# The last tile of a gated attention block, multiplied on GpSimd in halves and turned inside the products of the tile ahead

## The chip, the cores and the metric

The kernel runs on one core of a Trainium2 chip. The metric is device time in microseconds (us) of one execution: 338.8 us median of three runs (338.32 to 339.88).

## The reference, cut to what matters

2048 tokens of width 256 pass through a gated cross attention (16 heads of 64, 64 keys) and then a mixture of 16 experts, two per token, at most 320 rows an expert:

```python
x = x + tanh(g_xattn[0]) * xattn(layernorm(x), ctx, gamma, beta, Wq, Wkv, Wo, bo, mask)
x = x + tanh(g_ffn[0]) * ffn(layernorm(x), gate_w, w1, w2)

def ffn(x, gate_w, w1, w2):          # capacity 320, sentinel = 16 * 320
    probs = sigmoid(xf @ gate_w.T)
    top_vals, sel = top_k(probs, 2)
    weights = top_vals / (top_vals.sum(-1, keepdims=True) + 1e-06)
    onehot = one_hot(sel.reshape(-1), E)
    ranks = take_along_axis(cumsum(onehot, axis=0), flat_sel[:, None], axis=1)[:, 0] - 1
    valid = ranks < capacity
    slot = where(valid, flat_sel * capacity + ranks, sentinel)
    padded = zeros((sentinel + 1, d)).at[slot].set(repeat(xf, 2, axis=0))[:sentinel].reshape(E, capacity, d)
    h = gelu(einsum('ecd,edf->ecf', padded, w1))
    out_padded = einsum('ecf,efd->ecd', h, w2).reshape(sentinel, d)
    return (where(valid, out_padded[slot], 0) * weights).reshape(T, 2, d).sum(1)
```

## The kernel before

The tokens are 16 tiles of 128 rows, numbered 0 to 15 (`LAST` is 15), and 8 pairs of tiles (`PAIRS`). The order of every engine is written out by hand; engines wait for each other on counting semaphores. A loop of steps (`steps`) runs tiles through a pipeline: in step s tile s is scored, tile s-1 gets its softmax factors, tile s-2 is turned and multiplied with the values, tile s-3 gets its residual, its second norm and its gate. After step 15 a tail, written out, brings tiles 13, 14 and 15 through. The experts follow, and TensorE (PE) is fed in them by three products of float32r halves (high and low parts) for every exact one.

Of one tile in the tail, in order:

- `normalise` (line 492, POOL) multiplies the exponentials `probs` by `norm`, the inverse row sums; for tile 15 this is line 1047, on DVE.
- `turn_probs` (1217, PE) turns them into `ps_pT`; `copy_probs` (606, ACT) takes the high part, `low_probs` (968, DVE) the low part of each half.
- `attend` (1269, PE) makes 24 products into `ps_out`; between them `router` (1256) of the tile ahead.
- `first_residual` (978, DVE) makes `x1`; `second_stats` (986) its mean and variance; `second_norm` (468 to 470, POOL) the inverse deviation and the shift, in three instructions that wait for each other.
- `turn_x1` (1248, PE), `copy_x1` (622, ACT) and `router` give the logits; `gate_exp` (630, ACT) takes their exponentials, scaled by the inverse deviation; `second_rows` (615, ACT) writes the normalised rows `z2`.
- `begin`, `find`, `choose`, `place` (991 to 1026, DVE) find the two experts of each row; `counts` and `count_one` (1283 to 1295, PE) give the ranks. Tiles 12 and 13 (pair 6) go together, tile 14 and tile 15 each alone.
- `dispatch` (460, POOL) sends the rows to `padded` in DRAM by indirect DMAs, 4 for a pair. SP fetches an expert's rows back (378 to 381) when all of them have landed.

PE then issues 40 filler matmuls (1193, `keep_busy(40)`), turns the first expert's rows (1354), issues 8 more fillers and starts the first product (1370). ACT and DVE split the first weights meanwhile; DVE's first of these waits for `rows_sent` (540), POOL's mark behind its last dispatch.

## Time and profile before

| what | value |
|---|---|
| median of the runs | 338.8 us (338.32 to 339.88) |
| the profiled execution | 339.9 us, span 338.2 us |
| mean granted clock of PE | 0.968 of full |
| busy share of PE, DVE, ACT, POOL | 91%, 74%, 61%, 57% |
| end of step 15's products, start of the first expert product | 155.5 us, 188.7 us |

All positions below are in us from the span's start. In the timelines a row stands for one instruction or several alike ("x12"), with the time from the first's start to the last's end; the idle time ahead of it and what ended it follow in brackets. Matmuls overlap, so the next row can start before the one above ends. PEclk 0.50 is 1.2 GHz, 1.00 is 2.4 GHz.

### The profile page before, as it was taken

The page shows a single profiled execution, that of the slowest core. Times are in us where ns is not written, and L with a number is a line of the kernel's source. Part 1 is how long each engine was busy: PE and PEld are TensorE (multiplying, and loading weights), DVE is VectorE, ACT ScalarE, POOL GpSimd, SP SyncE. Part 2 cuts the span into 40 slices and gives each one's busy share as a digit, 9 for nine tenths or more (in the row PEclk, how much of TensorE's full clock was granted, in tenths as well). Part 3 has the DMA queues.
Part 4 walks back from the last instruction along what each step waited for, and adds up shares of the span by engine and source line. Part 5 has one row for each costly group of instructions (what it writes and reads, how often), then busy time and mean ns, then how long its engine had stood idle before and what let it go on. Part 6 is the DMA issues. An engine that isn't in the chain of part 4 may idle for free. (4 is left out here: it accounts for less than half of the span.)

```text
span 338.2 us, 6265 instructions
## 1 busy us (share of the span) xinstructions
PE 308.3 (91%) x2077; PEld 267.3 (79%) x2080; DVE 251.2 (74%) x585; ACT 207.9 (61%) x570; POOL 191.4 (57%) x242
## 2 busy tenths in 40 slices
PE   8989999999999999998849999999999999999800
PEld 3646779988888888887724899999999999999700
DVE  2679887698989898989755398888888888887200
ACT  2646877887888888866461376666666666665300
POOL 8034566585777777788771023555555555566650
PEclk9999999999999999999978999999999999999965
DMA  6989999700111111111224737878787878853440
GB/s 159 274 241 292 182 167 152 195 19 16 49 49 55 57 57 64 56 51 62 78 95 149 249 104 201 204 205 208 204 216 211 224 202 220 211 82 43 48 46 8
DMA packets 40906, 45.68 MB, mean 135 GB/s; under 512 B 5461, under 2 KB 34666, under 8 KB 40874
## 3 DMA queue, kind: packets, MB, share of 16 engines
q1 hardware_dynamic: 33410, 35.78, 39.3%
q0 software_dynamic: 7424, 9.48, 15.6%
q8 instruction: 17, 0.28, 0.4%
q14 instruction: 15, 0.12, 0.2%
q10 hardware_dynamic: 40, 0.02, 0.0%
HBM read 28.02 MB, written 17.24 MB: 134 GB/s over the span
## 5 line engine op out<-in xcount | busy, mean ns | idle before, releaser
L554 POOL DMA_INDIRECT out_dram<-wqT,diag x48 | 73.3, 1528 | 77.4 <-DMA out_dram<-wqT,diag 43.4
L1370 PE MATMUL ps_scores<-value_t,score_t 128*128 128x320 f32 x384 | 59.1, 310 | 0.0
L1370 PEld LDWEIGHTS ps_scores<-value_t,score_t 128*128 128x128 f32 x384 | 56.5, 188 | 0.4 <-DVE value_t L1079 0.3
L1269 PE MATMUL ps_out<-value_t,pT 128*128 128x256 f32 x384 | 53.3, 289 | 0.9 <-DVE pT L968 0.9
L1240 PE MATMUL ps_scores<-score_t,xn 128*128 128x512 f32 x192 | 53.9, 426 | 0.0
L1269 PEld LDWEIGHTS ps_out<-value_t,pT 128*128 128x128 f32 x384 | 47.7, 189 | 1.7 <-issue 1.6
L1240 PEld LDWEIGHTS ps_scores<-score_t,xn 128*128 128x128 f32 x192 | 36.4, 190 | 6.8
L713 ACT ACTIVATE ps_scores<-ps_scores 128x640 f32<-128x640 f32 x30 | 20.6, 688 | 34.2 <-PE ps_scores L1370 34.1
L460 POOL DMA_INDIRECT padded<-z,slot_row x32 | 33.4, 1043 | 10.0 <-issue 7.1
L640 ACT ACTIVATE probs<-ps_scores,row_low 128x64 f32<-128x64 f32 x128 | 38.0, 327 | 0.5 <-DVE row_low L941 0.5
L1093 DVE CAST value_t<-ps_scores 128x640 fp32r<-128x640 f32 x30 | 24.7, 824 | 18.0 <-ACT ps_scores L713 17.8
L492 POOL TENSOR_TENSOR probs<-probs,norm 128x1024 f32<-128x1024 f32 x15 | 28.6, 1906 | 5.5 <-DVE norm L909 5.5
L640 ACT ACTIVATION_READ_ACCUMULATOR probs<-ps_scores,row_low 128x1 f32 x128 | 28.4, 222 | 0.0
L848 DVE TENSOR_TENSOR pT<-ps_pT,pT 128x512 fp32r<-128x512 f32 x28 | 18.5, 660 | 5.2 <-ACT pT L606 4.9
L1095 DVE TENSOR_TENSOR value_t<-ps_scores,value_t 128x512 fp32r<-128x512 f32 x30 | 20.8, 692 | 1.0
L1106 DVE TENSOR_TENSOR score_t<-raw,score_t 128x1024 fp32r<-128x1024 f32 x16 | 19.4, 1216 | 2.6 <-POOL sent L540 2.6
L1193 PE MATMUL ps_misc<-zeros 128*128 128x512 bf16 x62 | 18.8, 461 | 1.5 <-DVE zeros L805 1.2
L1079 DVE TENSOR_TENSOR value_t<-ps_pT,value_t 128x640 fp32r<-128x640 f32 x16 | 13.1, 816 | 8.2 <-ACT value_t L701 8.2
L606 ACT ACTIVATE pT<-ps_pT 128x512 fp32r<-128x512 f32 x32 | 18.0, 644 | 0.9 <-PE ps_pT L1217 0.9
L701 ACT ACTIVATE value_t<-ps_pT 128x640 fp32r<-128x640 f32 x16 | 11.3, 706 | 11.9 <-PE ps_pT L1354 11.7
L630 ACT ACTIVATE gexp<-ps_scores,l 128x16 f32<-128x16 f32 x16 | 4.4, 276 | 22.3 <-PE ps_scores L1256 16.7
L483 POOL CAST xn<-xn_full 128x256 fp32r<-128x256 f32 x16 | 6.4, 399 | 20.6 <-ACT xn_full L654 20.5
(210 smaller groups left out, 690.0 us busy)
## 6 DMA issues: line engine op xcount, KB each, us to landing
raw<-in_L_ffn_w_dram SPq DMA_DIRECT2D x16, 512.0 KB, 4.8
wo_sb<-in_L_ffn_w_dram SPq DMA_DIRECT2D x16, 512.0 KB, 3.5
padded<-empty SPq DMA_DIRECT2D x2, 2064.0 KB, 31.0
diag<-padded SPq DMA_DIRECT2D x16, 258.0 KB, 4.9
out_dram<-x SPq DMA_DIRECT2D x16, 128.0 KB, 1.7
padded<-empty SPq DMA_DIRECT2D x1, 1032.0 KB, 34.1
diag<-padded SPq DMA_DIRECT2D x16, 64.5 KB, 4.7
wq_sb<-in_L_xattn_Wq_dram SPq DMA_DIRECT2D x2, 512.0 KB, 8.0
```

The costliest lines, as they stand in the source:

```text
L460: pool.indirect_dma_start(padded, bass.IndirectOffsetOnAxis(ap=slot_row[:, r % 2, k, q:q + 1], axis=0), z2[:, (2 * r + k) % RING, q], None ...
L492: pool.tensor_tensor(probs[:, p], probs[:, p], norm[:, p, :, None].to_broadcast([P, HEADS, KEYS]), ALU.mult).then_inc(normed, 1)
L554: pool.indirect_dma_start(out, bass.IndirectOffsetOnAxis(ap=xg[0:SLOTS[k], r, k, TOKEN:TOKEN + 1].bitcast(U32), axis=0), y[0:SLOTS[k], j, ...
L640: op = act.activation(probs[:, j, n], ps_scores[:, 1, at:at + KEYS], ACT.Exp, scale=-1.0, bias=row_low[:, n:n + 1], accum_out=row_sum[:, j ...
L713: act.activation(h_at(t, h), ps_scores[:, 2 * h:2 * h + 2, 0:CAPACITY], ACT.Gelu).then_inc(h_act, 1)
L1093: dve.tensor_copy(h_high_of(p)[:, fs], h_at(t, h)).then_inc(h_high, 1)
L1095: dve.tensor_tensor(h_low_of(p)[:, fs], h_at(t, h)[:, :, 0:n], h_high_of(p)[:, fs, 0:n].bitcast(F32), ALU.subtract)
L1106: dve.tensor_tensor(w1_hl(p, 1), raw1[:, p], w1_hl(p, 0).bitcast(F32), ALU.subtract).then_inc(w1_low, 1)
L1193: pe.matmul(ps_misc[:, :], idle_rows[:, 0:P], idle_rows, start=True, stop=True)
L1240: op = pe.matmul(dst, xn[:, t % 2, a, c], mv, start=False, stop=last)
L1269: op = pe.matmul(ps_attn, pT[:, a, c], mv, start=c == 0 and (a, b) == PARTS[0], stop=c == HC - 1 and (a, b) == PARTS[-1])
L1370: op = pe.matmul(ps_scores[:, f, 0:CAPACITY], w1_hl(p, a)[:, c, f * P:(f + 1) * P], x_hl(p, b)[:, c], start=c == 0 and (a, b) == PARTS[0], ...
```

## The change

- Tile 15's multiply moves from DVE (one of 1024 columns) to POOL (two of 512), each half with its own inverse and factor.
- Tile 15 is turned between the products 4 and 5 of tile 14's eight groups, into a buffer of its own (`score_t`), and its products go to a bank of their own (`ps_misc`), so that they needn't wait for tile 14's residual. The counts of pair 6 stand ahead of tile 14's last group. The router of tile 13 stands ahead of tile 14's products. Fillers go from 5 and 3 to 2.
- From tile 12 on the second norm is on three engines: DVE makes -mean and variance + eps (two instructions more behind its aggregate), POOL only the power, ACT the product (`shift`, a 128x1 activation) ahead of `second_rows`.
- On DVE the residual of tile 14 moves behind pair 6's places, the weights behind the choice (`weigh`), that of tile 15 behind `find`.
- POOL's dispatches stand in another order around the norms and multiplies.
- The 64 rows of expert 0's third block are fetched on ACT's DMA queue; the 0.5 KB rest has a semaphore of its own (`tailed`) for which PE doesn't wait.

```diff
+        pT_last = score_t[:, 0:2 * HC * P].rearrange("p (k c n) -> p k c n", k=2, c=HC)
+        shift = sb("shift", [P, 2, 1])
-        ps_attn = ps_out[:, 0:DIM]
+        def attn_of(t):
+            return ps_misc[:, 0:DIM] if t == LAST else ps_out[:, 0:DIM]
+        LATE_TILE = 2 * LATE_PAIR + 2
...
@@ sync: fetch(e)
-                    sp.dma_start(xg[0:SLOTS[2], r, 2], padded[at + 2 * P:at + CAPACITY, :]).then_inc(fetched[r], 16)
-                    sp.dma_start(xg[SLOTS[2]:, r, 2, TOKEN:], padded[at + 2 * P:at + CAPACITY, TOKEN:]).then_inc(fetched[r], 16)
+                    if e > 0:
+                        sp.dma_start(xg[0:SLOTS[2], r, 2], padded[at + 2 * P:at + CAPACITY, :]).then_inc(fetched[r], 16)
+                    sp.dma_start(xg[SLOTS[2]:, r, 2, TOKEN:], padded[at + 2 * P:at + CAPACITY, TOKEN:]).then_inc(tailed[r], 16)
...
@@ gpsimd: second_norm(t)
                 pool.wait_ge(stats2_ready, t + 1)
+                if t >= LATE_TILE:
+                    pool.tensor_tensor(l2[:, p, 1:2], l2[:, p, 0:1], power[:, 0:1], ALU.pow).then_inc(ln2_ready, 1)
+                    return
...
+            def last_multiply(h):
+                p, at = LAST % 2, 8 * h
+                pool.wait_ge(norm_ready, TILES + h)
+                pool.tensor_tensor(probs[:, p, at:at + 8], probs[:, p, at:at + 8],
+                                   norm[:, p, at:at + 8, None].to_broadcast([P, 8, KEYS]), ALU.mult).then_inc(normed, 1)
...
@@ scalar: second_rows(t)
+                if t >= LATE_TILE:
+                    bias = shift[:, p]
+                    act.activation(bias, l2[:, p, 2:3], ACT.Copy, scale=l2[:, p, 1:2]).then_inc(shifted, 1)
+                    act.wait_ge(shifted, t - LATE_TILE + 1)
...
@@ scalar: expert(e), e == -1
+                    for k in range(2):
+                        act.wait_ge(dispatched[k], 64 * PAIRS // 2)
+                    act.dma_start(xg[0:SLOTS[2], 0, 2], padded[2 * P:CAPACITY, :]).then_inc(fetched[0], 16)
...
@@ vector
+            def second_stats(t):
+                p = t % 2
+                done.sync()
+                dve.wait_ge(z2_ready, t - 1)
+                done.done(dve.bn_aggr(mv2[:, p], stats2[:, :]))
+                dve.tensor_scalar(l2[:, p, 2:3], mv2[:, p, 0:1], -1.0, None, ALU.mult)
+                dve.tensor_scalar(l2[:, p, 0:1], mv2[:, p, 1:2], EPS, None, ALU.add).then_inc(stats2_ready, 1)
...
+            def last_norm(h):
+                p, at = LAST % 2, 8 * h
+                done.done(dve.reciprocal(row_inv[:, at:at + 8], row_sum[:, p, at:at + 8]))
+                dve.wait_ge(normed, LAST - 1)
+                nan = nan_row[:, LAST % PER_BATCH:LAST % PER_BATCH + 1]
+                dve.tensor_scalar(norm[:, p, at:at + 8], row_inv[:, at:at + 8], nan, None, ALU.add).then_inc(norm_ready, 1)
...
@@ tensor, the tail
-            keep_busy(5)
-            attend(LAST - 1, {HC // 2: lambda: router(LAST - 2)})
-            turn_probs(LAST)
-            counts(PAIRS - 2)
-            turn_x1(LAST - 1)
-            keep_busy(3)
-            attend(LAST, {HC // 2: lambda: router(LAST - 1)})
+            keep_busy(2)
+            router(LAST - 2)
+            attend(LAST - 1, {HC // 2: lambda: turn_probs(LAST), HC - 1: lambda: counts(PAIRS - 2)})
+            attend(LAST, {3: lambda: turn_x1(LAST - 1), HC - 2: lambda: router(LAST - 1)})
```

On TensorE, from tile 14's products to tile 15's, before (`ps_scores<-ident,x` is `turn_x1`, `ps_scores<-small_t,wq_sb` the router):

```order
L1269 MATMUL ps_out<-value_t,pT 128x256 x12
L1256 MATMUL ps_scores<-small_t,wq_sb 128x16 x2
L1269 MATMUL ps_out<-value_t,pT 128x256 x12
L1217 MATMUL ps_pT<-ident,probs 128x128 x8
...
L1248 MATMUL ps_scores<-ident,x 128x128 x2
L1193 MATMUL ps_misc<-zeros 128x512 x3
L1269 MATMUL ps_out<-value_t,pT 128x256 x12
L1256 MATMUL ps_scores<-small_t,wq_sb 128x16 x2
L1269 MATMUL ps_out<-value_t,pT 128x256 x12
```

And the same stretch now (the counts are left out in both):

```order
L1317 MATMUL ps_scores<-small_t,wq_sb 128x16 x2
L1331 MATMUL ps_out<-value_t,pT 128x256 x12
L1278 MATMUL ps_pT<-ident,probs 128x128 x8
L1331 MATMUL ps_out<-value_t,pT 128x256 x9
...
L1331 MATMUL ps_out<-value_t,pT 128x256 x3
L1331 MATMUL ps_misc<-value_t,score_t 128x256 x9
L1309 MATMUL ps_scores<-ident,x 128x128 x2
L1331 MATMUL ps_misc<-value_t,score_t 128x256 x9
L1317 MATMUL ps_scores<-small_t,wq_sb 128x16 x2
L1331 MATMUL ps_misc<-value_t,score_t 128x256 x6
```

The eight turns of tile 15 moved from behind tile 14's products to their middle, and `turn_x1` of tile 14 from ahead of tile 15's products to behind their ninth.

On GpSimd, from the norm of tile 13 to the last dispatch, before (`padded<-z,slot_row` is one dispatch):

```order
L468 TENSOR_TENSOR l<-mv,eps_c 128x1
L469 TENSOR_TENSOR l<-l,power 128x1
L470 TENSOR_SCALAR l<-mv,l 128x1
L460 DMA padded<-z,slot_row 32768x258 x3
L453 TENSOR_TENSOR z<-token,zeros 128x4 x2
...
L460 DMA padded<-z,slot_row 32768x258 x4
...
L460 DMA padded<-z,slot_row 32768x258 x4
L540 MEMSET sent 128x1
```

And now (`L546` is half of tile 15's multiply, `L481` a norm's power):

```order
L546 TENSOR_TENSOR probs<-probs,norm 128x512
L481 TENSOR_TENSOR l<-l,power 128x1
L546 TENSOR_TENSOR probs<-probs,norm 128x512
L473 DMA padded<-z,slot_row 32768x258 x3
...
L473 DMA padded<-z,slot_row 32768x258
L481 TENSOR_TENSOR l<-l,power 128x1
L473 DMA padded<-z,slot_row 32768x258 x2
L481 TENSOR_TENSOR l<-l,power 128x1
L473 DMA padded<-z,slot_row 32768x258 x5
L568 MEMSET sent 128x1
```

Behind tile 15's norm, the last one, stand five dispatches where four stood.

## Rows read from the trace of the kernel before

**Rows 1.** The page's 40 slices of 8.5 us: tenths busy of PE, granted clock.

```profile
PE   8989999999999999998849999999999999999800
...
PEclk9999999999999999999978999999999999999965
```

**Rows 2.** Busy time by stretch: engines in us, then PEclk, DMA share, GB/s.

```profile
172.00:175.00 3.00, 0.00 (x1) 0.03 (x2) 1.63 (x11) 2.16 (x3) 2.18 (x4) 0.72 0.18 66
```

**Rows 3.** Timeline of PE, 158 to 190 us: start, duration, instruction, idle time and releaser.

```profile
158.86 1.66 PE L1269 MATMUL ps_out<-value_t,pT 128*128 128x256 f32 x12 [0.39 <-DVE pT L968]
...
162.24 1.04 PE L1217 MATMUL ps_pT<-ident,probs 128*128 128x128 f32 x8
...
165.67 1.66 PE L1269 MATMUL ps_out<-value_t,pT 128*128 128x256 f32 x12 [0.47 <-DVE pT L968]
167.23 0.62 PE L1256 MATMUL ps_scores<-small_t,wq_sb 128*128 128x16 f32 x4
...
175.00 0.17 PE L1294 MATMUL ps_scores<-running,ones_b 128*128 128x16 bf16 x1 [3.21 <-DVE both L1010]
...
175.05 4.86 PE L1193 MATMUL ps_misc<-zeros 128*128 128x512 bf16 x11
180.12 6.21 PE L1193 MATMUL ps_misc<-zeros 128*128 128x512 bf16 x28 [0.22 <-issue]
186.18 0.86 PE L1354 MATMUL ps_pT<-ident,diag 128*128 128x128 f32 x6
...
188.69 2.02 PE L1370 MATMUL ps_scores<-value_t,score_t 128*128 128x320 f32 x12
```

**Rows 4.** Timeline of DVE, 159 to 175 us.

```profile
159.23 1.22 DVE L1047 TENSOR_TENSOR probs<-probs,norm 128x1024 f32<-128x1024 f32 x1
161.27 0.18 DVE L991 TENSOR_SCALAR gden<-gexp 128x32 f32<-128x32 f32 x1 [0.82 <-ACT gexp L630]
...
163.79 0.48 DVE L978 SCALAR_TENSOR_TENSOR x<-ps_out,tgates,x_all 128x256 f32<-128x256 f32 x1
...
166.48 0.69 DVE L968 TENSOR_TENSOR pT<-ps_pT,pT 128x512 fp32r<-128x512 f32 x1
...
169.39 0.48 DVE L978 SCALAR_TENSOR_TENSOR x<-ps_out,tgates,x_all 128x256 f32<-128x256 f32 x1 [0.18 <-PE ps_out L1269]
...
174.66 0.19 DVE L1010 TENSOR_REDUCE both<-chosen 128x16 bf16<-128x32 bf16 x1
```

**Rows 5.** Timeline of POOL, 159 to 179 us.

```profile
159.33 2.05 POOL L460 DMA_INDIRECT padded<-z,slot_row  x1 [0.16 <-issue]
...
171.58 0.20 POOL L468 TENSOR_TENSOR l<-mv,eps_c 128x1 f32<-128x1 f32 x1
171.86 0.57 POOL L469 TENSOR_TENSOR l<-l,power 128x1 f32<-128x1 f32 x1
...
173.20 1.06 POOL L460 DMA_INDIRECT padded<-z,slot_row  x1 [0.42 <-issue]
...
176.16 0.95 POOL L460 DMA_INDIRECT padded<-z,slot_row  x1 [0.63 <-DVE slot_row L1023]
177.42 0.96 POOL L460 DMA_INDIRECT padded<-z,slot_row  x1 [0.30 <-issue]
```

**Rows 6.** Timeline of ACT at 172 us: the gate of the last tile.

```profile
172.82 0.27 ACT L630 ACTIVATE gexp<-ps_scores,l 128x16 f32<-128x16 f32 x1 [2.02 <-POOL l L470]
```

**Rows 7.** Timeline of POOL, then below of DVE, at 146 us.

```profile
145.62 1.90 POOL L492 TENSOR_TENSOR probs<-probs,norm 128x1024 f32<-128x1024 f32 x1
...
146.73 0.83 DVE L948 TENSOR_SCALAR gden<-gexp 128x32 f32<-128x32 f32 x1 [1.07 <-ACT gexp L630]
```

**Rows 8.** Timeline of SP's DMA queue at 180 us, and the landing of line 378's next transfer.

```profile
180.19 0.38 SPq L378 DMA_DIRECT2D diag<-padded  x1
180.62 0.48 SPq L380 DMA_DIRECT2D diag<-padded  x1
...
DMA to landing us min/median/max: 2.9/2.9/2.9
```

More of the change, by code:

```diff
@@ L20 @@
 TILES = TOKENS // P
+LAST = TILES - 1
 PER_BATCH = SEQ // P
@@ L273, in build @@
         fetched = [sem(f"fetched{k}") for k in range(GATHERS)]
+        tailed = [sem(f"tailed{k}") for k in range(GATHERS)]
         added = [sem(f"added{k}") for k in range(2)]
@@ L598, in _, with copy_probs @@
                 job(n, *JOBS[n])
-            def copy_probs(t):
-                for h in range(2):
+            def copy_probs(t, halves=(0, 1)):
+                for h in halves:
                     act.wait_ge(turned, 2 * t + h + 1)
-                    if h == 0:
+                    if t == LAST:
+                        act.wait_ge(scored, 2 * TILES)
+                    elif h == 0:
                         wait(act, attended, t)
-                    act.activation(pT[:, 0, 4 * h:4 * h + 4].rearrange("p c n -> p (c n)"), ps_pT[:, h],
+                    act.activation(pT_of(t, 0)[:, 4 * h:4 * h + 4].rearrange("p c n -> p (c n)"), ps_pT[:, h],
                                    ACT.Copy).then_inc(p_high, 1)
@@ L891, in step @@
                 if exists(t3):
-                    wait(dve, ln2_ready, t3 - 1)
-                    dve.bn_aggr(mv2[:, p3], stats2[:, :]).then_inc(stats2_ready, 1)
+                    if t3 < LATE_TILE:
+                        wait(dve, ln2_ready, t3 - 1)
+                        dve.bn_aggr(mv2[:, p3], stats2[:, :]).then_inc(stats2_ready, 1)
+                    else:
+                        second_stats(t3)
                 if route:
@@ L1058, in _ @@
             low_probs(LAST, 1)
+            first_residual(LAST - 1)
+            second_stats(LAST - 1)
             begin(PAIRS - 1, 0, 1)
+            find(0, 1)
             first_residual(LAST)
-            find(0, 1)
-            second_stats(LAST)
             link.sync()
             choose(PAIRS - 1, 0, 1)
+            second_stats(LAST)
+            weigh(PAIRS - 1, 0, 1)
             counts_of_one(0)
@@ L1071, in _ @@
             choose(PAIRS - 1, 1, 2)
+            weigh(PAIRS - 1, 1, 2)
             counts_of_one(1)
@@ L1213, in turn_probs @@
                 for h in range(2):
+                    if t == LAST and h == 1:
+                        pe.wait_ge(normed, TILES + 1)
                     wait(pe, p_low, 2 * (t - 1) + h + 1)
@@ L1259, in attend @@
             def attend(t, between):
-                wait(pe, x1_ready, t)
+                if t < LAST:
+                    wait(pe, x1_ready, t)
                 for c in range(HC):
@@ L1268, in attend @@
                         mv = value_w[b][:, batch_of(t), c]
-                        op = pe.matmul(ps_attn, pT[:, a, c], mv, start=c == 0 and (a, b) == PARTS[0],
+                        op = pe.matmul(attn_of(t), pT_of(t, a)[:, c], mv, start=c == 0 and (a, b) == PARTS[0],
                                        stop=c == HC - 1 and (a, b) == PARTS[-1])
@@ L1314, in step @@
                 if counted_here and r >= LATE_PAIR:
-                    between[HC - 2] = lambda: counts(r)
+                    between[HC // 2 + 1] = lambda: counts(r)
                 if exists(s - 2):
```

70 lines of the change are left out of this document (37 added, 33 removed).

## The prediction

> **What bounds the kernel now.** I read the page's slices first [rows 1]: TensorE is the full engine nearly everywhere and dips once, in the slices from 152 to 178 us (8, 8 and 4 tenths), where attention ends and the experts begin. There the granted clock dips too, and not again before the end. The table of stretches says it in numbers [rows 2]: from 172 to 175 us PE is not busy at all, at a mean clock of 0.72. From 178 us on PE shows nine tenths or more in every slice until the last three. What follows 188.7 us is PE alone, so the end of the program moves with the start of the first expert product, and with nothing else.
>
> Then I followed that start backwards in the timelines. The first product starts at 188.69, 2.5 us behind the turn of expert 0's rows at 186.18 (ACT's and DVE's copies of these rows, beside eight fillers) [rows 3]. The turn follows the 40 fillers without a gap. They start at 175.05, right behind the last count: 11 records in 4.86 us (0.44 each, half clock) and 28 in 6.21 (0.21 each, full clock; one of the 40 has no record). The rows themselves were ready before: SP asked for them at 180.19, and the next transfer of that kind took 2.9 us to land [rows 8], so about 183.1. So the fillers, not the rows, set the turn, with some 3 us to spare for the rows.
>
> The last count waited 3.21 us for DVE's choice for tile 15 [rows 3], whose chain started with the gate at 172.82 [rows 6]; that gate waited for POOL's norm, begun at 171.58 [rows 5]. Its input was there earlier: x1 of tile 15 was made at 169.39 to 169.87 [rows 4]. Between lie DVE's statistics (about 0.7 us) and POOL's dispatches, which stand ahead of the norm. So the present chain is: tile 15's products, x1, norm, gate, choice, count, fillers, turn.
>
> **The change part by part.** Times are those of this execution.
>
> *1. The start of the tail.* Ahead of tile 14's products DVE gets more to do: two small instructions behind each of two aggregates (tiles 12 and 13), an inverse and a factor for the second half, six in all with the waits between them. A small DVE instruction takes 0.18 us, as at 161.27 [rows 4]: six are 1.1 us. Some overlap, some wait an extra 0.05. I take 1.0 (bounds 0.5 and 1.6): products from 158.86 to 159.9. POOL's earlier token marks (0.2 each) hide behind PE, which is full until 155.5.
>
> *2. Tile 15 turned inside.* Twelve products take 1.5 us (158.86 to 160.36, the router's place in between). So the turns start at 161.4 instead of 162.24 [rows 3]. The multiply on POOL is ready by then: it is DVE's 1.22 us [rows 4] no more, and half of POOL's 1.90 for 1024 columns [rows 7] is 0.95, begun at about 157.5 and 159.4. Tile 14's 24 products, 8 turns (0.9) and 5 counts (0.15) end 4.05 us after 159.9, at 163.95, and tile 15's products follow at once (its first low half is ready at about 163.3, 0.7 each for ACT's copy and DVE's low part, as at 166.48 [rows 4]). Before they started at 165.67. This is a lead of 1.7 us.
>
> *3. The lead is spent on x1 of tile 14.* Nine products later, at 165.05, PE comes to `turn_x1` of tile 14, and its x1 now stands behind pair 6's places and the second low half on DVE. Before, DVE went from 161.27 to 167.17 (the end of that low half) [rows 4], of which x1 and statistics of tile 14 took 1.1, now moved behind. The rest, 4.8 us, begins at 160.4 now (1.0 later by step 1, 1.2 and 0.8 of idle time earlier, the gate being ready) and waits about 0.3 for the turned half: x1 starts at 165.5 and ends at 166.0, where it ended at 164.27. PE stalls for 1.0 us. With 3 and 6 products more (1.15 with the turn) the router of tile 14 comes at 167.4, before at 167.23 [rows 3]. So the gate of tile 14 is at best where it was; I carry +0.15. Behind it DVE makes begin and find (1.2 us) and then x1 of tile 15, at 169.5 (before 169.39). The bounds: -0.4 if DVE is a little quicker, then PE's products are the next limit; +1.0 if step 1 costs its upper end.
>
> *4. The norm of tile 15.* This is where time is won. DVE: x1 until 170.0, statistics 0.43, then the choice's two (0.4), the aggregate and the two small ones, 0.5: 171.2. POOL stands ready, since only two dispatches (1.27 apart, from 176.16 and 177.42 [rows 5]) lie between the norms, where three stood. Its one power takes 0.57 [rows 5], so the gate comes at 171.9 instead of 172.82: -0.9. Two thirds of it are the two instructions gone from POOL (1.2 us from 171.58 to the gate, now 0.7 with the wait), the rest the queue. Bounds: -1.4 (with step 3's lower bound) and +0.1.
>
> *5. To the turn.* Gate to count is unchanged (2.18 us), so the fillers start at 174.15 and, with the same clock, take the same 11.1 us: turn at 185.3, -0.9.
>
> *6. POOL's last dispatches.* Five instead of four stand behind the norm: 171.9, 0.4 of start (as 172.78 to 173.20), five at 1.27: the last ends at about 178.5, before at 178.38 [rows 5]. The rows gain nothing, and ACT's product `shift` (0.2 us) falls into this time too. Cover: rows ready at 183.2 against fillers until 185.3. If that cover goes, the rows are late next.
>
> *7. Two queues for expert 0.* SP's second request starts 0.43 us behind the first and takes 0.48 [rows 8], and the third comes behind it; ACT's queue saves one, and the rest is not waited for. All of it lies under the fillers: 0. If the fillers ended first it would be worth up to 0.9.
>
> *8. Locks between DVE and POOL.* In rows 7 a small DVE instruction, 0.18 elsewhere, took 0.83 and ended at 147.56, as POOL's multiply ended (147.52). The other way, a dispatch at 159.33 took 2.05 beside DVE's multiply at 159.23 [rows 4, 5] where others take 0.96. So the move of the multiply frees POOL of 1.1 and puts DVE's small instructions at risk, under two half multiplies instead of none. POOL's half at 157.5 runs beside x1 and statistics of tile 13, the other beside two low halves that read PSUM; I charge 0, bounds 0 and 1.9 (both halves whole).
> The Trainium skill ("GPSIMD Engine Reference", section "Key points") says that GpSimd shares its SBUF interfaces with VectorE and contends with DVE instructions in a 2-port mode or with two SBUF inputs. Rows 7 bear it out. By this rule x1, with one operand in PSUM, and the low parts pass freely, and `norm` and the two new scalar instructions are at risk; by it alone the upper bound is not reached, since the larger instructions pass.
>
> Sum: -0.9 us. The profiled execution, 339.9 us, would become 339.0. It is 1.1 over the median of the runs. The fillers can account for that: 11 of them at half clock cost 0.23 each more than at full, 2.5 us in all, and an execution in which the clock comes back sooner is faster by a part of that. So I take the difference from the median: 338.8 - 0.9 = 337.9.
>
> **The rivals.** 0.5% is 1.7 us, about what this kernel's measurement can tell from no change.
>
> *The rows become the limit, and the clock stays up.* PE now has fewer gaps (the wait of 3.2 becomes about 2.3 us), so the clock may not fall. Then 40 fillers take 8.6 us, end at 182.75, and the turn waits for the rows at 183.2, which dispatches and queues set: 3.0 us less than 186.18, so 339.9 - 3.0 = 336.9. For it: the mean clock of 0.72 over 172 to 175 [rows 2] says that it fell only inside that stretch. Against: PE has again some 5 us from 169 with hardly a matmul.
>
> *DVE is late throughout: slower.* Place: x1 of tile 14, before which DVE carries all that was added. From the point where x1 ends past 166.0, every delay goes through router and gate to the fillers one to one, while step 4 returns 1.05. With the locks' 1.9 added to step 3 the turn is at 186.2 + 1.0: 338.8 + 1.0 = 339.8. For it: DVE has no idle time left in step 3. Against: rows 7 show the lock for a single small instruction only.
>
> *Nothing arrives.* The norm of tile 15 gains 0.9, but x1 is 0.9 later (step 1 at 1.6 and no overlap): 338.8. That the products come 1.7 us sooner would then be seen, and the count at 175.0 as before.
>
> *More is won.* Step 3 at its lower bound and DVE's choice ahead: the turn 1.8 earlier, 337.0.
>
> **How the numbers follow.** The forecast, fillers set the turn and start 0.9 earlier: 0.50, its own range 337.2 to 338.5. Clock stays up: 0.15. More is won: 0.10. Nothing arrives: 0.13. DVE late: 0.12. Faster by over 0.5% (below 337.1): the second and third, mostly, and a tail of the first, 0.27. Slower by over 0.5% (above 340.5): only the outer part of the last, 0.06. The same: 0.67. The range for 8 in 10: 336.7 to 339.2, which takes in the clock's case and the case of no gain and leaves out the outer part of DVE late.
>
> **What would show it.** Products of tile 15 at about 164.0, with a stall of 1 us in them for x1 of tile 14; router of tile 14 at 167.2 to 167.6; the power for tile 15 at 171.3 and its gate at 171.9; the last count at 174.1; fillers at two clocks; the last dispatch at 178.5; the turn at 185.3, right behind the fillers. I am wrong if the turn waits for the rows (step 6), if small DVE instructions last 0.5 us or more (step 8), or if the gate of tile 14 is off 168.1 by more than half a microsecond (step 3).

## The result and the profile after

| kernel | median us | span | outside the span | ratio to before, 95% |
|---|---|---|---|---|
| before | 339.49 (338.29 to 341.62) | 337.8 (e1) | 1.74 (e1) | 1 |
| the changed kernel | 342.07 (339.54 to 343.89) | 339.95 | 1.91 | 1.007 [1.0054, 1.0086] |

The change makes the kernel 0.7% slower, some 2.4 us. The forecast was 337.9 us with a range up to 339.2, so it was wrong, and on the wrong side. Executions in a slower state (for the changed kernel 355.7 and 363.5 us) are left out of every median here. The profiled execution of the changed kernel took 341.69 us, with a span of 339.3. Spans of one kernel scatter: those of the kernel before from 336.6 to 338.5 (29 runs taken beside e1), those of the changed one from 337.7 to 341.9. The span and the time outside it that the table gives for before are of the repeated measurement e1.

The page's slices of the changed kernel, tenths busy of PE, then the granted clock. They answer to [rows 1]:

```profile
PE   8989999999999999997759999999999999999600
...
PEclk9999999999999999999959999999999999999965
```

The dip is shallower (7, 7, 5 where it was 8, 8, 4), as forecast. Behind it nothing can be told apart in PE's row but the last slices, and there lies the first lesson: PE is idle in the last 17 us (18 in the changed kernel), and that end is another engine's. The timeline of PE in the changed kernel (start, duration, instruction, idle time and releaser), against [rows 3]:

```profile
157.73 0.44 PE L1309 MATMUL ps_scores<-ident,x 128*128 128x128 f32 x2 [1.42 <-DVE x L1031]
...
159.72 1.66 PE L1331 MATMUL ps_out<-value_t,pT 128*128 128x256 f32 x12 [0.46 <-DVE pT L1021]
...
163.74 1.23 PE L1331 MATMUL ps_misc<-value_t,score_t 128*128 128x256 f32 x9
166.89 0.44 PE L1309 MATMUL ps_scores<-ident,x 128*128 128x128 f32 x2 [1.92 <-DVE x L1031]
...
168.68 1.63 PE L1331 MATMUL ps_misc<-value_t,score_t 128*128 128x256 f32 x6
...
175.63 0.17 PE L1356 MATMUL ps_scores<-running,ones_b 128*128 128x16 bf16 x1 [2.34 <-issue]
175.68 10.30 PE L1252 MATMUL ps_misc<-zeros 128*128 128x512 bf16 x40
185.82 0.86 PE L1413 MATMUL ps_pT<-ident,diag 128*128 128x128 f32 x6
...
188.34 1.88 PE L1429 MATMUL ps_scores<-value_t,score_t 128*128 128x320 f32 x11
```

The first expert product starts at 188.34, 0.35 us before the 188.69 of [rows 3]. The span ends 1.1 us later all the same. The rows of GpSimd tell where this went. Its scatter-adds (`out_dram<-wqT,diag`, indirect DMAs that add an expert's rows to the output) go three to an expert, and the first of each three waits until the adds of the expert ahead have landed. In the kernel before, first their line on the page (busy time, mean of one; idle time and what ended most of it), then adds of the second expert and of the last two:

```profile
L554 POOL DMA_INDIRECT out_dram<-wqT,diag x48 | 73.3, 1528 | 77.4 <-DMA out_dram<-wqT,diag 43.4
```

```profile
211.82 1.55 POOL L554 DMA_INDIRECT out_dram<-wqT,diag  x1 [5.50 <-DMA out_dram<-wqT,diag]
...
316.51 1.56 POOL L554 DMA_INDIRECT out_dram<-wqT,diag  x1 [2.55 <-DMA out_dram<-wqT,diag]
...
320.24 1.42 POOL L554 DMA_INDIRECT out_dram<-wqT,diag  x1 [0.30 <-DMA out_dram<-wqT,diag]
324.07 1.56 POOL L554 DMA_INDIRECT out_dram<-wqT,diag  x1 [2.40 <-issue]
...
327.81 1.42 POOL L554 DMA_INDIRECT out_dram<-wqT,diag  x1 [0.30 <-issue]
```

And the last ones of the changed kernel:

```profile
321.15 1.44 POOL L583 DMA_INDIRECT out_dram<-wqT,diag  x1 [0.30 <-issue]
325.26 1.56 POOL L583 DMA_INDIRECT out_dram<-wqT,diag  x1 [2.67 <-DMA out_dram<-wqT,diag]
...
328.99 1.43 POOL L583 DMA_INDIRECT out_dram<-wqT,diag  x1 [0.30 <-issue]
```

PE's last matmul starts at 320.6 in both. The last expert's adds start 3.5 and 4.7 us behind it, since they wait for those landings, as the adds of all 15 experts behind the first do in both kernels. (The view of before names a landing for the first 14 of them and none for the last, whose wait of 2.40 us is as long; in the changed kernel it names one there, 2.67.) Three issues 1.87 apart and a landing make a period of 7.5 to 7.8 us at best, and single periods of 8.4 us and more stand in every trace, where a landing took longer. The first period is always the longest, 11.19 us before (200.63 to 211.82, behind a wait of 5.50) and 10.99 in the changed kernel. The other 14 take 8.02 us each before ((324.07 - 211.82) / 14) and 8.14 in the changed kernel, against 8.21 of PE (24 products of an expert to those of the next). So the chain falls behind PE by its first period and is too slow to catch up by the end, and the prediction never looked at it.

### The profile page after: what moved, and what is told of

Read it like the earlier page. It is cut to its first block, busy times and chain, and to the rows that moved or that the text cites. A ratio compares the mean times of both kernels' runs of the same rounds, so it can differ in the third digit from the quotient of the medians.

```text
span 339.3 us, 6307 instructions
## 1 busy us (share of the span) xinstructions
PE 307.6 (91%) x2074; PEld 267.6 (79%) x2074; DVE 252.0 (74%) x594; ACT 209.4 (62%) x574; POOL 191.0 (56%) x236
## 4 chain that ended last, share of the span: by engine, by line
PE 75%; POOL 6%; DVE 6%; ACT 4%; issue 3%; DMA 2%; SPq 0%; DVEq 0%; POOLq 0%; ACTq 0%
PE ps_scores L1429 17%; PE ps_scores L1301 10%; PE ps_out L1331 9%; PE ps_out L1447 7%; PE ps_misc L1447 6%; PE ps_misc L1252 4%; PE ps_pT L1413 3%; PE ps_pT L1278 3%; PE ps_out L1458 2%; PE ps_out L1457 2%; ACT probs L676 2%; POOL out_dram L583 2%; PE ps_scores L1295 2%; PE ps_scores L1317 1%; DMA wkv_b<-in_L_xattn_Wkv_dram 1%
## 5 line engine op out<-in xcount | busy, mean ns | idle before, releaser
L1331 PE MATMUL ps_out<-value_t,pT 128*128 128x256 f32 x360 | 50.2, 289 | 0.5 <-DVE pT L1021 0.5
L1331 PEld LDWEIGHTS ps_out<-value_t,pT 128*128 128x128 f32 x360 | 44.8, 189 | 0.6 <-issue 0.5
L473 POOL DMA_INDIRECT padded<-z,slot_row x32 | 32.4, 1013 | 10.5 <-issue 8.0
L1252 PE MATMUL ps_misc<-zeros 128*128 128x512 bf16 x59 | 16.6, 440 | 1.2 <-DVE zeros L846 1.2
L637 ACT ACTIVATE pT<-ps_pT 128x512 fp32r<-128x512 f32 x30 | 17.1, 642 | 0.0
L763 ACT ACTIVATE score_t<-raw 128x1024 fp32r<-128x1024 f32 x16 | 16.8, 1056 | 0.3
```

The source lines that it names most:

```text
L473: pool.indirect_dma_start(padded, bass.IndirectOffsetOnAxis(ap=slot_row[:, r % 2, k, q:q + 1], axis=0), z2[:, (2 * r + k) % RING, q], None ...
L1252: pe.matmul(ps_misc[:, :], idle_rows[:, 0:P], idle_rows, start=True, stop=True)
L1331: op = pe.matmul(attn_of(t), pT_of(t, a)[:, c], mv, start=c == 0 and (a, b) == PARTS[0], stop=c == HC - 1 and (a, b) == PARTS[-1])
```

## The experiments

The letters of the theories change on the way. In the expectations of e1 to e4, A is that the tail costs the time, B that the chain of adds sets the end, C that it lies outside the span. In those of e5 to e8, D is the address of the new tile and E the second queue. From e9 on, A is the chain (the end is set by the adds, so a lead or a delay of the first product arrives there changed) and B the tail (the end follows the first product, and the tail itself is late in most executions). e13 to e15 have a C and a D of their own, told there. Each ratio is to runs of the kernel before taken beside the experiment on the same chip, whose medians were 339.60 us for e1 to e4, 339.49 for e5 to e8 and 339.16 for e9 to e16.

**e1, e2: both kernels again.**

> The kernel before, unchanged: how far two executions of one kernel lie apart, in the span and in what lies outside of it. In the two profiled executions at hand the changed kernel starts the first expert product 0.35 us earlier and yet ends its span 1.1 us later, with 2.4 us outside of the span instead of 1.7. Theory A (the tail between attention and experts costs the 2.4 us of the medians): spans of this kernel about 338 us, with 1.7 to 1.9 outside. Theory B (the end of the program, GpSimd's chain of scatter-adds, varies by a microsecond or more in any kernel and decides): spans scatter from 336.5 to 339.5 and their end is set by the landings of the adds. Theory C (time outside of the span): 1.7 outside here, 2.4 in the changed kernel.

> The changed kernel, unchanged, for a second trace on the same chip as the others. Theory A: again some 2 to 2.6 us over the kernel before; DVE waits again about 0.9 us for the counts of pair 6, x1 of tile 14 ends at about 166.8, and the last count starts at 175.6. If the wait of 0.9 us was an accident of one execution, x1 ends at 166.0 and the last count starts at about 174.7. Theory B: the ratio holds, but the place of the first expert product doesn't tell it.

e1: 339.55 us, ratio 0.9999 [0.9981, 1.0016]. e2: 341.45 us, 1.0054 [1.0032, 1.0075]. The loss is real. The profiled execution of e2 took 349.97 us and lost its time in the experts' part, so it is read only up to the first product. Timeline of PE in e2:

```profile
166.13 0.44 PE L1309 MATMUL ps_scores<-ident,x 128*128 128x128 f32 x2 [0.86 <-DVE x L1031]
167.48 0.52 PE L1317 MATMUL ps_scores<-small_t,wq_sb 128*128 128x16 f32 x4
...
174.00 0.17 PE L1356 MATMUL ps_scores<-running,ones_b 128*128 128x16 bf16 x1 [2.42 <-DVE both L1057]
174.05 11.51 PE L1252 MATMUL ps_misc<-zeros 128*128 128x512 bf16 x40
185.40 0.86 PE L1413 MATMUL ps_pT<-ident,diag 128*128 128x128 f32 x6
```

This is the tail as forecast (router 167.4, count 174.1, turn 185.3), to 0.1 us. So the same code gives this tail in one execution and the one above in another.

**e3: tile 14's residual earlier.** In the changed kernel, on DVE:

```diff
             weigh(PAIRS - 2, 0, 2)
+            first_residual(LAST - 1)
+            second_stats(LAST - 1)
+            low_probs(LAST, 1)
             counts_of(PAIRS - 2)
             place(PAIRS - 2, 0, 2, PAIRS - 1)
-            low_probs(LAST, 1)
-            first_residual(LAST - 1)
-            second_stats(LAST - 1)
```

> The changed kernel with tile 14's residual and statistics ahead of pair 6's counts and places and of tile 15's second low half on DVE. Theory A with the stall of 1.9 us in tile 15's products as its main cost: the stall goes, x1 of tile 14 ends at 164.5, the router of tile 14 waits for the second low half instead and comes at about 166.9 to 167.4 instead of 168.2; 0.8 to 1.2 us less than the changed kernel, about 341.0. Theory B: no change, 342.

341.70 us, 1.0059 [1.0033, 1.0085]: nothing gained. In its profile twelve products of tile 14 take 2.90 us in place of 1.66, at half clock, and the first product starts at 190.01. The stall for x1 of tile 14 went (166.59, no wait), but pair 6's places came later, and POOL's dispatch, which stands ahead of tile 14's norm and needs them, waited 4.31 us, to 169.11. So the edit moved the wait more than it removed it, and it doesn't test what the stall costs.

**e4: the fetch as before.** The changed kernel with expert 0's 64 rows on SP's queue and one semaphore again.

```diff
-                    if e > 0:
-                        sp.dma_start(xg[0:SLOTS[2], r, 2], padded[at + 2 * P:at + CAPACITY, :]).then_inc(fetched[r], 16)
+                    sp.dma_start(xg[0:SLOTS[2], r, 2], padded[at + 2 * P:at + CAPACITY, :]).then_inc(fetched[r], 16)
```

> The changed kernel with the fetches of the expert rows as in the kernel before: all three transfers on SP's queue and on one semaphore, nothing on ACT's queue. Theory A: the fetch lies under the fillers, so no difference to the changed kernel (342.1, within 0.4 us). Theory B, if the extra waits or the second queue slow the chain of adds (their waits for a landing were 2.6 to 3.1 us instead of 2.4): 1 to 2 us less, 340 to 341. Theory C, if the five semaphores more lengthen what lies outside of the span: 0.5 us less, all of it outside.

340.42 us, 1.0022 [0.9996, 1.0048]: 1.0 us below e2 by the medians, but the two intervals overlap, so that a gain is likely and not shown.

**e5, e6, e8: the place of the new tile.** `shift` moves 20 tiles behind it by 32 bytes. In e5 it is declared last, in e8 too with e4's fetch (the tail alone), and e6 is the kernel before with an unused tile in its place.

```diff
         l2 = sb("l2", [P, 2, 3])
+        spare = sb("spare", [P, 2, 1])
```

> The changed kernel with its one new SBUF tile, shift (8 bytes a partition), declared last, so that every other tile lies where it lay in the kernel before. In the changed kernel it moved 20 tiles by 32 bytes, among them raw1 and w2_third (weights), from a multiple of 64 bytes to 32 beside one; the twelve products with w2_third took 1.60 instead of 1.57 us, and all products from the first expert's on 0.23 us more. Theory D (the addresses cost the time): about 1 to 2 us less than the changed kernel, span near 338.3. Theory A (longer tail) or E (the second queue and its semaphores alone): no change, span 339.6.

> The kernel before with an unused tile of 8 bytes a partition where the changed kernel has shift: the addresses of the changed kernel and nothing else of it. Theory D: 0.7 to 2 us slower than the kernel before, 340.3 to 341.6, products with w2_third at 1.60 us. The others: as the kernel before, 339.6.

> The changed kernel with both taken back: shift declared last and the fetches as in the kernel before. What is left is the rewritten tail. In two of three undisturbed traces it starts the first expert product 0.8 us earlier. If D and E together carry the loss: 0.3 to 0.9 us faster than the kernel before, 338.7 to 339.3. If the chain of scatter-adds sets the end whatever the tail does: the same as before, 339.6. If the tail itself costs: above 340.

e5: 341.24 us, 1.003 [0.9999, 1.0062]. e6: 339.78, 1.0013 [0.9996, 1.003]. e8: 340.88, 1.0047 [1.0028, 1.0067]. PE's period per expert is 8.228 us in the four traces with the shifted tiles (the changed kernel, e3, e4, e6) and 8.211 in before, e1, e5, e7 and e8, which makes 0.3 us from the first product to PE's last matmul (132.2 against 131.9). That is small, and not told from zero in the time (e6). The tail alone costs 0.5%, within 0.3 to 0.7. e5 has the second queue on top of e8 and is not slower by the ratios, whose intervals overlap.

**e7: two queues in the kernel before.** The edit of `fetch` and of `expert` of the change, alone.

> The kernel before with the changed fetch alone: expert 0's 64 rows on ACT's queue and the 0.5 KB rest on semaphores of its own. Theory E (this part costs what lies between the changed kernel and the one with a single queue): 1.0 us more in the span and 0.2 to 0.3 more outside of it, 340.8. Theory D: no change, 339.6; then the 1.1 us between these two kernels were an interaction or noise.

340.24 us, 1.003 [1.0016, 1.0045], slower by 0.75. In its profile the clock came back sooner (40 fillers in 10.19 us, 11.29 in e1), the first product started at 187.48, 1.2 us ahead of before, and the last expert's adds at 323.64, 0.4 ahead. This is the first experiment to show a lead that arrives only in part.

**e9, e10, e11: the chain taken away.** The odd experts' adds go to another DRAM tensor, so that the adds of neighbours needn't be ordered, in the kernel before (e9), the changed one (e10) and the tail alone (e11). These three kernels, and e13 to e15 below, leave out the sum of the two tensors: the odd experts' share is missing in the output. The edit changes two things at once, the wait and the target.

```diff
+    other = nc.dram_tensor("other", [TOKENS + DUMMY, DIM], F32, kind="Internal").ap()
...
-                wait(pool, added[(j + 1) % 2], SLOT_TILES * 16 * (i + j))
+                wait(pool, added[j], SLOT_TILES * 16 * i)
...
-                    pool.indirect_dma_start(out, bass.IndirectOffsetOnAxis(
+                    pool.indirect_dma_start(other if j else out, bass.IndirectOffsetOnAxis(
```

> The kernel before, with one thing left out: the scatter-adds of the odd experts go to a DRAM tensor of their own, so the odd experts' share is missing in the output, and an expert's adds no longer wait for the landing of the adds of the expert ahead, only for those of two experts ahead. Theory A (the end of the program is set by GpSimd's chain of adds, which lags behind TensorE when a landing is slow): little changes in the kernel before, whose chain lagged by about 0.5 us at the end: span 337.2 to 337.6 at the median, where the kernel before has 337.8, and the spans lie closer together than its 336.6 to 338.5. Theory B (the chain has nothing to do with it, the adds follow TensorE anyway): span unchanged at 337.8, spread unchanged.

> The changed kernel with the same thing left out (odd experts' adds to a tensor of their own). Theory A: what the changed kernel loses is lost in the chain of adds. Without the chain the end follows the first expert product, which is 0.35 to 0.8 us earlier than in the kernel before; TensorE's longer period gives 0.2 back and the time outside the span 0.2 to 0.3: 0.0 to 0.5 us below the same edit of the kernel before, where the whole kernels stand 2.3 us apart. Theory B (the loss is in TensorE's own path, in a tail that stalls in some executions): 1.5 to 2.3 us above the same edit of the kernel before, and the first product of its profile starts later than 189.

> The tail of the change alone (one DMA queue for expert 0's rows as before, the new 8 byte tile placed last), with the odd experts' adds to a tensor of their own. Theory A: 0.4 to 0.9 us below the same edit of the kernel before, which is what the prediction had forecast for the tail. Theory B: 0.9 to 1.4 above it, as the tail alone stood above the kernel before.

| | median us | spans | ratio to before |
|---|---|---|---|
| e9 | 334.88 | 333.1 (332.5 to 334.0) | 0.9861 [0.9823, 0.99] |
| e10 | 335.71 | 333.9 (333.5 to 335.0) | 0.9897 [0.9861, 0.9932] |
| e11 | 335.83 | 334.0 (333.5 to 336.1) | 0.9908 [0.9874, 0.9943] |

e9 and before are the plainest pair of the study. The first product starts at 188.70 in e9 and at 188.69 in before; the spans are 334.0 and 338.2. POOL's adds in e9, of the second expert and of the last two:

```profile
208.77 2.15 POOL L555 DMA_INDIRECT other<-wqT,diag  x1 [2.43 <-ACT wqT L730]
...
314.65 1.56 POOL L555 DMA_INDIRECT out_dram<-wqT,diag  x1 [2.16 <-ACT wqT L730]
...
320.12 1.57 POOL L555 DMA_INDIRECT other<-wqT,diag  x1 [0.30 <-issue]
...
323.86 1.42 POOL L555 DMA_INDIRECT other<-wqT,diag  x1 [0.30 <-issue]
```

In 14 of 15 rounds the wait now names ACT's result (PE's work), where it named a landing; the last round has no wait, and the last add is 3.95 us sooner. Of this, 1.86 us is the lag that the chain already has at the last expert but one (316.51 against 314.65), and 2.09 is the last round itself, 7.56 us against 5.47. The chain of adds costs 4.2 us in the kernel before. I had expected 0.5: I had not seen that even without a slow landing the last expert's adds must wait for those of the one ahead. Between the changed kernel (339.3) and e10 (333.8), whose products start at 188.34 and 188.25, the chain costs 5.5. That is 1.3 us more, but from one pair of profiles, and the 15 rounds scatter by as much: 123.4 us in before, 124.9 in the changed kernel, 123.2 in e8 and 125.5 in e4, which both have the one queue. So it isn't shown that the change lengthens the chain. Without the chain the changed kernel is 0.8 us above e9 by the medians, with intervals that overlap, and neither theory had that size: A expected e10 and e11 below e9, B 0.9 to 2.3 above. e10 and e11 are alike, so that queue and address cost nothing there that these few runs tell.

**e12: 30 fillers for 40 in the kernel before.** `keep_busy(40)` becomes `keep_busy(30)`.

> The kernel before with 30 fillers in place of 40 behind the last count, nothing left out. The turn of expert 0's rows comes ten fillers of 0.21 us sooner, at 184.1 in place of 186.2, as the rows are there at 183.1, and the first product at 186.6. If the end moves with the first expert product and with nothing else, as the prediction said: 2.1 us faster, 337.4. Theory A: the chain of adds takes back a part, as with two queues in the kernel before, where the product came 1.2 us sooner and the last add 0.4: 0.3 to 1.0 us faster.

339.02 us, 0.9993 [0.9962, 1.0023]. Its PE, then a piece of its chain of waits:

```profile
183.25 0.92 PE L1354 MATMUL ps_pT<-ident,diag 128*128 128x128 f32 x6 [0.37 <-DMA diag<-padded]
...
185.82 2.03 PE L1370 MATMUL ps_scores<-value_t,score_t 128*128 128x320 f32 x12
```

```profile
320.45 2.42 issue
322.87 1.56 POOL out_dram L554
```

The first product comes 2.87 us sooner and PE's last matmul 2.83, the last expert's adds 1.20, and the median moves by 0.1 us. So the lead goes through PE whole, and the chain takes 1.7 us of it back in this profile: its 15 rounds took 125.1 us here and 123.4 before. The first add starts 11.94 to 11.98 us behind the first product in every trace, so the chain does start sooner; why its landings then take longer is open. The opening claim of the prediction had promised 2.1 or more. e12 also shows the turn waiting for the rows (0.37, landed at about 183.2): the rows are late next where the prediction had put them.

**Why the tail is late: e13 to e16.** Without the chain an execution ends 145.3 us behind its first product (145.3, 145.55 and 145.3 in e9 to e11), so these kernels measure when the first product starts. In e11's profile PE waits for x1 of tile 13, and then this follows:

```profile
158.42 0.44 PE L1302 MATMUL ps_scores<-ident,x 128*128 128x128 f32 x2 [1.44 <-DVE x L1025]
...
160.41 2.90 PE L1324 MATMUL ps_out<-value_t,pT 128*128 128x256 f32 x12 [0.46 <-DVE pT L1015]
163.10 1.16 PE L1271 MATMUL ps_pT<-ident,probs 128*128 128x128 f32 x8
```

Two stretches of e11 in busy time (PE, PEld, DVE, ACT, POOL, then PEclk, DMA share, GB/s), and below the first of them in e9:

```profile
158.00:163.00 5.00, 4.08 (x20) 3.51 (x21) 4.48 (x20) 2.31 (x6) 4.18 (x5) 0.69 0.20 72
160.00:162.00 2.00, 1.59 (x7) 1.62 (x8) 1.79 (x8) 1.27 (x3) 1.82 (x2) 0.50 0.00 0
```

```profile
158.00:163.00 5.00, 4.61 (x38) 4.20 (x36) 3.90 (x14) 2.06 (x5) 4.05 (x6) 1.00 0.15 54
```

The same products take 2.90 us at 1.2 GHz that take 1.66 at 2.4. Before, PE waited 0.42 us for this x1 and had five fillers behind it; now it waits 1.4 us, with two. In five of eight profiles of the changed tail (e3, e5, e8, e10, e11) the clock fell there, in none of six of before's tail. In the changed kernel's own it fell later, behind the wait of 1.92 us (PEclk 0.63 from 168 to 170 us, 0.50 from 170 to 173.5). Theory C: the wait that the change made on PE ahead of tile 14's products lets the clock fall, in part of the executions, and this costs up to 1.5 us (from the start of tile 14's products to that of tile 15's: 5.56 us in e3, 4.02 in the changed kernel). Rival D: DVE's added work makes the tail late, whatever the clock. In e13 to e15 the adds are in two tensors, as in e9.

e13, the tail of e11 with six fillers in that wait:

```diff
             turn_probs(LAST - 1)
+            keep_busy(6)
             turn_x1(LAST - 2)
```

> The tail of the change alone, odd experts' adds to a tensor of their own, and six fillers ahead of the turn of tile 13's x1, where TensorE waited 1.4 us. Theory C (that wait lets the granted clock fall at 159 us in part of the executions, and tile 14's products and tile 15's turns then take 1.3 to 1.6 us more): the clock stays full until 170 us, twelve products of tile 14 in 1.66 us, and the time is 0.8 to 1.4 us below the same tail without the fillers, at or a little below the same edit of the kernel before. Theory D (DVE's added work, not the clock, makes the tail late): unchanged or some tenths slower, since the turn of x1 may come behind the last filler.

333.83 us, 0.9848 [0.9835, 0.9861], 2.0 us below e11 and 1.05 below e9; all five runs (333.81 to 334.06) lie below all of both, though the interval overlaps that of e9. PE in e13:

```profile
156.51 1.46 PE L1245 MATMUL ps_misc<-zeros 128*128 128x512 bf16 x6
158.10 0.44 PE L1302 MATMUL ps_scores<-ident,x 128*128 128x128 f32 x2
...
160.09 1.66 PE L1324 MATMUL ps_out<-value_t,pT 128*128 128x256 f32 x12 [0.46 <-DVE pT L1015]
...
166.21 0.44 PE L1302 MATMUL ps_scores<-ident,x 128*128 128x128 f32 x2 [0.88 <-DVE x L1025]
...
186.75 2.03 PE L1423 MATMUL ps_scores<-value_t,score_t 128*128 128x320 f32 x12
```

Six fillers, which compute nothing, give 2.0 us. DVE's work is unchanged, so D falls as the cause of that time. More than the 1.5 us of the products is won: the spans, 333.5 to 336.1 in e11, are 332.1 to 332.3 in e13, and the clock is also back sooner behind the last count (40 fillers in 10.27 us, 11.08 in e11).

e14, the other way to take the wait away: on DVE `first_residual(LAST - 2)` and `second_stats(LAST - 2)` ahead of tile 15's row sum and `last_norm(0)`.

> The tail of the change alone, odd experts' adds to a tensor of their own, and on DVE the residual and statistics of tile 13 ahead of tile 15's row sum, inverse and factor, so that TensorE's wait for x1 of tile 13 falls from 1.4 to about 0.4 us. Theory C: no fall of the clock at 159 us, 0.8 to 1.4 us below the same tail without the edit. Theory D: also faster, by about the 1.1 us by which x1 of tile 13 comes sooner, but with no change of the clock. The first half of tile 15's multiply starts 1.2 us later and must still be ready for the turn at 161.

336.02 us, 0.9908 [0.9874, 0.9941], no gain over e11, against both theories' figures. PE in e14:

```profile
156.43 0.44 PE L1302 MATMUL ps_scores<-ident,x 128*128 128x128 f32 x2 [0.33 <-DVE x L1025]
...
160.30 2.90 PE L1324 MATMUL ps_out<-value_t,pT 128*128 128x256 f32 x12 [2.06 <-DVE pT L1015]
```

x1 comes sooner as expected, but DVE's work is the same, and PE's wait moved behind it, to the low part (0.46 to 2.06). The sum of the waits there grew from 1.90 us in e11 to 2.70, and the clock fell again, so the edit took no wait away and tests neither theory. Both had it faster, and both missed.

e15, the kernel of e9 without the five fillers ahead of tile 14's products:

```diff
             turn_x1(LAST - 2)
-            keep_busy(5)
```

> The kernel before, odd experts' adds to a tensor of their own, without the five fillers between the turn of tile 13's x1 and tile 14's products, so that TensorE is idle there for about 1.7 us beside the 0.4 us ahead of it. Theory C: the clock falls behind 158 us in part or all of the executions, the products of tile 14 take 1 us more or so, and the time is 0.5 to 1.6 us above the same kernel with the fillers. Theory D: unchanged within 0.3 us, or slightly faster, as nothing is done in that time but fillers.

335.42 us, 0.9895 [0.9873, 0.9918], 0.5 above e9, which the two intervals alone do not part. Its profile does:

```profile
158.67 2.65 PE L1270 MATMUL ps_out<-value_t,pT 128*128 128x256 f32 x12 [1.46 <-DVE pT L969]
```

With a wait in that place the kernel before loses the clock too: tile 14's products start where they do in e9 (158.67, 158.71), and the last count comes 1.3 us later (176.15, 174.84). The 40 fillers then took 10.38 us in place of 11.45, so that only 0.24 of it reached the first product.

e16, the tail of e8 with e13's fillers, whole:

> A whole kernel, nothing left out: the tail of the change alone (one DMA queue as before, the new tile placed last) with six fillers ahead of the turn of tile 13's x1. Theory A (the chain of adds sets the end): whatever the tail gains at the first expert product, the end does not move with it: within 0.3% of the kernel before, where the same tail without the fillers was 0.5% slower. If the end moved with the first product, and theory C holds: 0.5 to 1 us faster than the kernel before.

338.69 us against 339.16 of before, 0.9992 [0.9976, 1.0007]; e8 had 1.0047 [1.0028, 1.0067]. Its first product starts at 186.95, 1.7 us ahead of before, its last expert's adds at 322.68, 1.4 ahead, and the medians differ by 0.5 us, which the interval does not tell from nothing. This is the best version of the change that keeps the whole output. The fillers mend the tail's loss, clear of both intervals, in a whole kernel too. A gain over the kernel before isn't shown: in the profile 1.4 us of the lead arrive, in the medians 0.5 at most.

## Why the prediction was wrong

**The step that failed is the opening one**: "What follows 188.7 us is PE alone, so the end of the program moves with the start of the first expert product, and with nothing else." It was read off PE's busy slices. A full PE says that PE is never idle, not that the end is PE's: the page's last slices (PE 8, 0, 0 in [rows 1]) and the idle time of POOL's adds, 43.4 us of it ended by landings, stood there to be read. In its place the runs showed a chain of 15 landings behind PE: e9 moves the end by 4.2 us at an equal first product, and e12 starts the first product 2.87 us sooner and gains 0.1 in the median.

**Steps 1 and 2** held to 0.2 us: tile 14's products at 159.72 (159.9), tile 15's at 163.74 (163.95).

**But step 1 named only the lateness and not the wait that it makes.** "Products from 158.86 to 159.9" was right, and PE's wait for x1 of tile 13 grew from 0.42 to 1.42, with three fillers fewer behind it. The prediction looked for the clock in the long wait from 172 us alone, and one of its rivals had the clock stay up, because PE has fewer gaps. There are fewer, six in e2 from the turn of tile 13's x1 to the last count where before has eight, but their sum didn't fall (6.8 us, 6.6 before), and the one that counted grew. e13 shows it in the time and e15 in its profile. This term was put at nothing, and it decides the sign: the tail alone loses 0.5% without the six fillers (e8) and nothing with them (e16).

**Step 3** is right in e2 (166.13 for the turn of x1 with a stall of 0.86, router 167.48). In the changed kernel's own profile DVE waited 0.95 us more for the counts of pair 6, and the router came at 168.24. PE's last count ended at 163.44 and DVE went on at 164.70; in the other profiles it took up the counts without a wait, or right behind PE's (e14, 0.81 us). The cause is open.

**Steps 4 and 5** hold where step 3 does: power 171.14, gate 171.74, count 174.00, turn 185.40 in e2, forecast 171.3, 171.9, 174.1, 185.3. In the changed kernel's profile the last router ran at half clock:

```profile
172.25 1.03 PE L1317 MATMUL ps_scores<-small_t,wq_sb 128*128 128x16 f32 x4
```

It took 0.59 before, and gate (173.37) and count (175.63) are 1.5 late. The fillers took 10.30 us in place of 11.1, so the turn was 0.4 sooner than before.

**Step 6**: the last dispatch ends at 179.08 (177.99 in e2; forecast 178.5), and the turn waits for nothing. Right.

**Step 7**, two queues at 0: e7 shows a cost of 0.75 us [0.5, 1.5 by its interval], where the prediction had nothing or a gain. It does not lie in the tail, e10 and e11 show none of it without the chain, and e5 against e8 shows none either. In the changed kernel, e5 and e7 the shortest wait for a landing is 2.53 to 2.63 us, where the one-queue kernels have 2.35 to 2.42; e3, with two queues, has 2.43. So it seems to lie in the chain, but this is not shown.

**Step 8**, locks at 0: right in size, but by the order in time and not because the lock is absent. DVE's small instructions fell between POOL's halves, not beside them:

```profile
157.38 1.03 POOL L546 TENSOR_TENSOR probs<-probs,norm 128x512 f32<-128x512 f32 x1 [0.24 <-DVE norm L1091]
159.24 1.03 POOL L546 TENSOR_TENSOR probs<-probs,norm 128x512 f32<-128x512 f32 x1
```

```profile
158.39 0.15 DVE L882 TENSOR_SCALAR l<-mv 128x1 f32<-128x1 f32 x1
158.46 0.14 DVE L883 TENSOR_SCALAR l<-mv 128x1 f32<-128x1 f32 x1
158.75 0.23 DVE L1091 TENSOR_SCALAR norm<-row_inv,nan_row 128x8 f32<-128x8 f32 x1
```

The first half ended at 158.41 and the second began at 159.24. Beside the first stood x1 and the statistics of tile 13, at 0.48 and 0.43 us as ever, and beside the second the low parts. What the lock would cost `norm` and the two new instructions isn't tested here. Under POOL's whole multiply (153.20 to 155.11) a small DVE instruction still took 0.91 us in the changed kernel, where its like took 0.23 (163.53).

One slip in the sums: the rival in which the clock stays up was priced from the profiled execution (339.9 - 3.0 = 336.9) and the forecast from the median. From the median it would have been 335.8, outside the range that was said to take it in. It did not come.

The sum itself came out near, as a statement on the tail with its clock up: the last count is 0.8 us sooner in e13 than in e9 (174.07, 174.84; forecast 0.9), and the medians stand 1.05 apart. The second agreement is in part luck, since the two intervals overlap and e13's fillers also ran faster (10.27 us against 11.45). Two things outside the sum decided, the clock and the chain.

Of the 2.4 us lost, 1.6 are the tail's (e8 at 1.0047), and they go with the wait that grew: filled, the same tail loses nothing (e16 at 0.9992). The rest is small beside the scatter: e2, e3, e5 and e8 have overlapping intervals, the time outside the span gives 0.2, and what the queue costs comes out as 0.75 us (e7), 1.0 (e4 against e2, not clear of noise) or nothing (e5 against e8). What stays open: why single landings take up to 2 us longer, why the first round always does, and why a lead lengthens the rounds.

## What to carry over

Before asking what a stage's start is worth, follow the end back: look at which engine runs last, take the period of every loop-carried chain in the long stage (here adds that wait for the landing of the adds ahead, 7.5 us at best, 8.0 on average, 11.2 in the first round) and compare it with the full engine's (8.21). When the two are about as long, see which of them every round waits for: if it is the chain, a lead of the engine may be lost in it (1.7 of 2.87 us in e12's profile). When work is moved off the critical engine, list its new waits one by one, not their sum, and fill a wait that has grown: a rewrite that is right on paper lost 2.0 us (e11 against e13) to a clock that six empty matmuls kept up.

## What the runs showed of the hardware

- **The clock fell behind a wait that was not the longest.** At 159 to 160 us it went to 1.2 GHz behind PE's waits of 1.4 and 0.46 us in five of eight executions with the same instructions, and stayed at 2.4 GHz in the others. PE's longest wait, some 2.4 us ahead of the last count, came later. Where the clock could fall there, the times scattered: spans 333.5 to 336.1 (e11), 332.1 to 332.3 with the wait filled (e13).
- **A scatter-add's landing sets a floor.** POOL waits at least 2.35 us (e6) to 2.63 (e5), by the shortest wait of each trace, behind the last of three adds before the next may start, and up to 4.45 in single rounds (e8). The first round waits 5.2 to 5.8 us in every kernel that orders the adds; in e9 its second expert's adds start 8.12 us behind the first's, in before 11.19.
- **32 bytes of SBUF offset** make twelve products that read one moved tile 1.60 us long in place of 1.57 (period of an expert 8.228 against 8.211 us, in the changed kernel, e3, e4, e6 and e10 against the others). The addresses are those of the compiled program, not of a trace.
- **Time outside the span moves.** Its median is 1.74 or 1.75 us in before, 1.8 to 1.85 in kernels with the new tail, 1.9 to 2.05 in the changed kernel, e3 and e5, but 1.77 in e10, which has the second queue too, and 1.72 and 1.74 with the wait filled (e13, e16). What makes it is open.
